# A graph layer's routed messages in two float32r parts in place of three bf16 parts

## The reference

```python
h = x @ W_in2f
Wij = ssp(f_ij @ W_filt1 + b_filt1) @ W_filt2 + b_filt2     # ssp(v) = softplus(v) - ln 2
Wij = Wij * rcut_ij[:, None]
x_ij = h[idx_j] * Wij                                       # idx_j is dst
agg = segment_sum(x_ij, idx_i, num_segments=6250)           # idx_i is src, in no order
out = ssp(agg @ W_out1 + b_out1) @ W_out2 + b_out2
return layernorm(x + out)
```

## Time and profile before

| | |
|---|---|
| runs | 2374.13, 2367.33, 2362.75 us; median 2367.33 |
| span of the profiled execution | 2368.4 us, the only time given for it |
| PE / DVE / ACT / POOL busy | 2142.1 / 1670.5 / 1660.6 / 1862.0 us |
| PE matmul instructions | 16313 |
| granted TensorE clock, mean | 0.964 |
| DMA moved | 250.00 MB |
| chain that ended last, by engine | DMA 43%, PE 19%, POOL 17%, issue 14% |

### The profile page before, as it was taken

The page is one execution under the profiler, slowest core; times in us unless marked ns, Lnnn a source line. Parts: engine busy times, 40 slices in busy tenths (PEclk is TensorE's granted clock), DMA queues, the critical chain, the costliest instruction groups (busy, mean ns, idle before and its releaser), DMA issues.

```text
span 2368.4 us, 60320 instructions
## 1 busy us (share of the span) xinstructions
PE 2142.1 (90%) x16313; PEld 1410.6 (60%) x16313; DVE 1670.5 (71%) x3879; ACT 1660.6 (70%) x3725; POOL 1862.0 (79%) x1174
## 2 busy tenths in 40 slices
PE   2488999999999999999999999999999999999936
PEld 1365666566666666666666566666666666666613
DVE  5467777768676777767777777777777777777726
ACT  0277777678687777777776777877777777777616
POOL 2078888888888888888888888888888888888874
PEclk8599999999999999999999999999999999999978
DMA  6776665666666666666666666656666566666574
GB/s 208 267 155 95 96 95 90 93 90 100 94 99 92 100 97 95 92 98 97 93 98 93 94 94 94 102 94 96 96 98 91 93 100 95 95 96 91 68 159 130
DMA packets 370945, 250.00 MB, mean 106 GB/s; under 512 B 88788, under 2 KB 350143, under 8 KB 370315
## 3 DMA queue, kind: packets, MB, share of 16 engines
q0 software_dynamic: 160560, 73.14, 32.7%
q1 hardware_dynamic: 199482, 155.27, 27.3%
q10 hardware_dynamic: 10476, 16.77, 1.9%
HBM read 149.90 MB, written 95.13 MB: 103 GB/s over the span
## 4 chain that ended last, share of the span: by engine, by line
DMA 43%; PE 19%; POOL 17%; issue 14%; DVE 3%; ACT 3%; POOLq 0%; SPq 0%; DVEq 0%; ACTq 0%
DMA table<-total,index 40%; POOL table L732 16%; PE unit_psum L1872 5%; PE unit_psum L1891 4%; PE both_psum L1828 3%; PE total_psum L1841 2%; PE pre_psum L1815 2%; DMA h_parts<-h_out 1%; DMA src_g<-in_src 1%; PE both_psum L1853 1%; PE both_psum L1824 1%; ACT out_rows L1122 1%; DVE rank L1249 0%; DVE rank_part L1244 0%; POOL half_sum L776 0%
## 5 line engine op out<-in xcount | busy, mean ns | idle before, releaser
L732 POOL DMA_INDIRECT table<-total,index x1115 | 1803.3, 1617 | 444.8 <-issue 249.0
L1872 PE MATMUL unit_psum<-moving,route_hot 128*128 128x386 bf16 x3136 | 608.8, 331 | 41.0 <-ACT ring L915 36.9
L885 ACT ACTIVATE h_dst<-both_psum,cols 128x128 f32<-128x128 f32 x1564 | 450.2, 386 | 102.4 <-PE both_psum L1853 99.0
L1891 PE MATMUL unit_psum<-scat_hot,ring 64*128 64x448 bf16 x4704 | 481.7, 353 | 9.2 <-DVE scat_hot L1432 6.5
L1872 PEld LDWEIGHTS unit_psum<-moving,route_hot 128*128 128x128 bf16 x3136 | 295.0, 99 | 266.9 <-ACT ring L915 108.2
L915 ACT ACTIVATE ring<-unit_psum 128x386 bf16<-128x386 f32 x784 | 373.5, 509 | 111.8 <-PE unit_psum L1872 70.5
L1828 PEld LDWEIGHTS both_psum<-w_f,hidden 128*128 128x128 f32 x3128 | 415.3, 193 | 18.3
L1828 PE MATMUL both_psum<-w_f,hidden 128*128 128x128 f32 x3128 | 415.7, 276 | 0.0
L1891 PEld LDWEIGHTS unit_psum<-scat_hot,ring 64*128 64x128 bf16 x4704 | 217.0, 95 | 218.5 <-DVE acc_t L1448 7.7
L849 ACT ACTIVATE soft<-pre_psum 128x1024 f32<-128x1024 f32 x196 | 201.9, 1030 | 169.5 <-PE pre_psum L1815 168.6
L1841 PE MATMUL total_psum<-message,same 128*128 128x129 f32 x2232 | 309.5, 281 | 4.8 <-DVE message L1360 4.3
(11 more groups left out here) (116 smaller groups left out, 1599.7 us busy)
## 6 DMA issues: line engine op xcount, KB each, us to landing
dst_b<-dst SPq DMA_DIRECT2D x391, 128.0 KB
src_b<-src SPq DMA_DIRECT2D x279, 128.0 KB
f_t<-in_f_t SPq DMA_DIRECT2D x98, 256.0 KB
table<-total,index POOLq DMA_INDIRECT x1115
table<-zeros ACTq DMA_DIRECT2D x20, 640.0 KB, 5.7
window<-h_parts SPq DMA_DIRECT2D x391, 32.0 KB
parts<-table SPq DMA_DIRECT2D x48, 256.0 KB, 5.2
h_parts<-h_out SPq DMA_DIRECT2D x12, 384.0 KB, 5.4
```

The costliest lines, as they stand in the source:

```text
L732: pool.indirect_dma_start(tables[table], bass.IndirectOffsetOnAxis(index[:, i, k:k + 1], 0), total[:, i, k, 0:DIM], None, compute_op=ALU.a ...
L885: last = act.activation(h_dst[:, b, d], source, ACT.Copy, scale=cols[:, g[1] // HALF % 2, weight:weight + 1])
L1872: last = pe.matmul(unit_psum[:, k % 2, 0:MOVING], route_hot[:, tile, k * P:(k + 1) * P], moving[:, tile, :], start=(tile == 0), stop=(tile ...
L1891: last = pe.matmul(unit_psum[:, strip, 0:BUCKET], ring[rows, r[1] % RING, slot_tile(m), part * DIM:(part + 1) * DIM], scat_hot[rows, r[1] ...
```

## The change

The routed messages go in two float32r parts. [...] So `take_rest`, `split_mid` and `slot_nodes` go, `split_lo` subtracts `moving`'s first part from the message, and the node number travels as one float32r beside a zero. `MOVING` is 258 columns where it was 386. `ring`, `scat_hot`, `route_hot` and `moving` are float32r and take more room, so four buffers lie in the space of `x_rows`. Therefore x's rows are loaded when the last message is made and the last routing matmul is through, and VectorE waits for the zeroed tables before its first group. The order of the other calls stays as it is.

```diff
-MOVING = 3 * DIM + 2
+MOVING = 2 * DIM + 2
...
-        local_parts = sb("local_parts", [P, ROUTES, TILES, 2], BF16)
-        slot_node = sb("slot_node", [P, RING, SLOT_TILES], F32)
+        local_cols = sb("local_cols", [P, ROUTES, TILES, 2], F32)
...
-        ring = at(0, "ring", [P, RING, SLOT_TILES, MOVING], BF16)
-        scat_hot = at(37856, "scat_hot", [P, RING, BUCKET], BF16)
-        route_hot = at(44128, "route_hot", [P, TILES, SLOT_ROWS], BF16)
-        moving = at(51296, "moving", [P, TILES, MOVING], BF16)
-        message_r = at(54400, "message_r", [P, TILES, DIM], F32)
-        rest_r = at(56448, "rest_r", [P, TILES, DIM], F32)
+        ring = at(0, "ring", [P, RING, SLOT_TILES, MOVING], F32R)
+        scat_hot = at(50592, "scat_hot", [P, RING, BUCKET], F32R)
...
+        def before_x(offset, name, shape, dt):
+            return nc.alloc_sbuf_tensor_at(name, shape, dt, offset=x_rows_at + offset)
+
+        route_hot = before_x(0, "route_hot", [P, TILES, SLOT_ROWS], F32R)
+        moving = before_x(14336, "moving", [P, TILES, MOVING], F32R)
+        message_r = before_x(18464, "message_r", [P, TILES, DIM], F32)
+        h_dst = before_x(20512, "h_dst", [P, 2, GROUP], F32)
...
             def load_rows_of_x():
                 full = FULL_CHUNKS * CHUNK
-                sp.wait_ge(tables_zeroed, ZEROED)
+                sp.wait_ge(message_done, GROUPS)
...
-                if is_at(g, 2 * QUAD):
-                    load_rows_of_x()
...
             with sp.If(is_narrow):
                 run_groups(sp, step_narrow)
+                sp.wait_ge(route_mm_done, through_tile((0, ROUTES - 1), SLOT_TILES - 1))
+                load_rows_of_x()
                 for k in range(TABLES):
                     sp.wait_ge(table_added[k], adds_before((0, GROUPS - 1), plain, tiles_in((0, GROUPS - 1)), k))
...
-                act.activation(moving[:, :, 3 * DIM:MOVING],
-                               local_parts[:, bass.ds(PER_UNIT * r[0] + r[1], 1), :, :]
+                act.activation(moving[:, :, 2 * DIM:MOVING],
+                               local_cols[:, bass.ds(PER_UNIT * r[0] + r[1], 1), :, :]
                                .rearrange("p a k c -> p (a k) c"), ACT.Copy).then_inc(local_done, 1)
-
-            def split_mid(r):
...
-                dve.tensor_copy(local_parts[:, :, :, 0], nodes).then_inc(meta_step, 1)
+                dve.tensor_copy(local_cols[:, :, :, 0], nodes).then_inc(meta_step, 1)
                 steps += 1
-                dve.wait_ge(meta_step, steps)
-                dve.tensor_tensor(local_parts[:, :, :, 1], nodes, local_parts[:, :, :, 0], ALU.subtract
-                                  ).then_inc(meta_step, 1)
+                dve.memset(local_cols[:, :, :, 1], 0.0).then_inc(meta_step, 1)
...
                         dve.wait_ge(hi_done, through_routed(plus(r, -1)))
-                        dve.wait_ge(rest_done, through_routed(plus(r, -1)))
+                        dve.wait_ge(lo_done, through_routed(plus(r, -1)))
...
-            def take_rest(r):
...
-                dve.wait_ge(mid_done, through_routed(r))
-                dve.wait_ge(rest_done, through_routed(r))
-                dve.tensor_tensor(moving[:, :, 2 * DIM:3 * DIM], rest_r[:, :, :], moving[:, :, DIM:2 * DIM],
+                dve.wait_ge(hi_done, through_routed(r))
+                dve.tensor_tensor(moving[:, :, DIM:2 * DIM], message_r[:, :, :], moving[:, :, 0:DIM].bitcast(F32),
                                   ALU.subtract).then_inc(lo_done, 1)
...
-            def slot_nodes(r):
...
-                dve.wait_ge(node_done, through_routed(r))
+                dve.wait_ge(ring_done, through_tile(r, SLOT_TILES - 1))
...
-                                  slot_node[:, r[1] % RING, k:k + 1], None, ALU.is_equal).then_inc(hot_done, 1)
+                                  ring[:, r[1] % RING, k, 2 * DIM:2 * DIM + 1].bitcast(F32), None, ALU.is_equal
+                                  ).then_inc(hot_done, 1)
...
-                slot_nodes(r(-2))
                 finish_hidden(pair(1))
-                take_rest(r(-1))
+                split_lo(r(-1))
                 slot_one_hot(m(0), 6)
                 multiply(g(1), plain)
-                split_lo(r(-1))
...
             with dve.If(is_narrow):
+                dve.wait_ge(tables_zeroed, ZEROED)
                 run_units(dve, unit, rest)
...
+                    if is_at(c, 0):
+                        dve.wait_ge(x_rows_loaded, 32)
...
-                    pe.wait_ge(mid_done, through_routed(r))
...
-                for part in range(3):
+                for part in range(2):
                     for strip in range(STRIPS):
...
-                                         stop=final and part == 2)
+                                         stop=final and part == 1)
```

More of the change, by code:

```diff
@@ L76 @@
 assert LAST_UNIT < GROUPS <= LAST_UNIT + 7
-F32, BF16 = mybir.dt.float32, mybir.dt.bfloat16
+F32, BF16, F32R = mybir.dt.float32, mybir.dt.bfloat16, mybir.dt.float32r
 I32, U16 = mybir.dt.int32, mybir.dt.uint16
@@ L467, in build @@
         acc_zeroed = sem("acc_zeroed")
-        hi_done, rest_done, mid_done, lo_done = (sem(n) for n in ("hi_done", "rest_done", "mid_done", "lo_done"))
+        hi_done, lo_done = sem("hi_done"), sem("lo_done")
         local_done, route_hot_done, route_mm_done = sem("local_done"), sem("route_hot_done"), sem("route_mm_done")
-        ring_done, node_done, hot_done = sem("ring_done"), sem("node_done"), sem("hot_done")
+        ring_done, hot_done = sem("ring_done"), sem("hot_done")
         taken_done, acc_done = sem("taken_done"), sem("acc_done")
@@ L1411, in route_one_hot @@
                     hot.then_inc(route_hot_done, 1)
-            def slot_nodes(r):
-                if not routes(r):
-                    return
-                dve.wait_ge(ring_done, through_tile(r, SLOT_TILES - 1))
-                dve.tensor_tensor(slot_node[:, r[1] % RING, :], ring[:, r[1] % RING, :, 3 * DIM],
-                                  ring[:, r[1] % RING, :, 3 * DIM + 1], ALU.add).then_inc(node_done, 1)
             def slot_one_hot(m, x):
@@ L1488, in unit @@
                 route_one_hot(r(0), 2); route_one_hot(r(0), 3)
-                take_rest(r(0))
-                slot_nodes(r(-1))
+                split_lo(r(0))
                 slot_one_hot(m(1), 6)
                 finish_hidden(pair(3))
-                split_lo(r(0))
                 multiply(g(5), plain)
@@ L1512, in unit @@
                 compare_dst(g(10))
-                slot_nodes(r(0))
-                take_rest(r(1))
+                split_lo(r(1))
                 slot_one_hot(m(2), 6)
@@ L1540, in unit @@
                 multiply(g(11), plain)
-                take_rest(r(2))
-                slot_nodes(r(1))
+                split_lo(r(2))
                 compare_dst(g(14))
@@ L1565, in unit @@
                 route_one_hot(r(3), 0); route_one_hot(r(3), 1); route_one_hot(r(3), 2); route_one_hot(r(3), 3)
[L1566 to L1567 removed]
+                split_lo(r(3))
                 multiply(g(15), plain)
                 slot_one_hot(m(4), 6)
[L1570 removed]
                 mark_repeated(g(14), plain)
@@ L1591, in unit @@
                 multiply(g(18), plain)
-                take_rest(r(4))
-                slot_nodes(r(3))
+                split_lo(r(4))
                 compare_dst(g(21))
                 slot_one_hot(m(5), 6); slot_one_hot(m(6), 0); slot_one_hot(m(6), 1)
-                split_lo(r(4))
                 slot_one_hot(m(6), 2)
@@ L1616, in unit @@
                 compare_dst(g(24))
-                slot_nodes(r(4))
-                take_rest(r(5))
+                split_lo(r(5))
                 slot_one_hot(m(6), 6)
```

40 lines of the change are left out of this document (5 added, 35 removed).

## The result

The kernel after the change took 2394.35 us (median; 2387.63 to 2398.10), the kernel before, on the same chip, 2365.04. The ratio is 1.0112, with an interval of 1.0093 to 1.0132: slower, by more than the 0.5% that a measurement can tell from no change. The forecast was 2374 in a range from 2345 to 2405. The profiled execution's span is 2391.7 us against 2368.4, +23.3.

The account below looks back on a forecast made before the run. POOL's scatters were taken to bound the kernel: 19.3 (one-hots) - 8.4 (take_rest) - 5.6 (waits) + 1.4 (x's rows) = +6.7 us on 2367.3, forecast 2374. The range was 2345 to 2405, and 2353 to 2395 from its own bounds.

Parts of the forecast that it names:

- POOL paces the loop: Loop: POOL's 1115 scatters run one after the other, 0.30 us apart; PE, DVE and ACT wait for it through buffers.
- The one-hots' length: VectorE: float32r output lengthens slot one-hots by 58 ns and route one-hots by 170 ns, +122 us of DVE.
- The price of the growth: Scatters: blocking weight is count x duration squared, 0.160 us a unit; longer one-hots add 120.3 units, +19.3 us.
- take_rest's -8.4: VectorE: dropping take_rest removes blocking weight 52.2, so scatters shorten by 8.4 us.
- Waits of 5.6 us that would close: Gaps between scatters: a PE that catches up sooner closes POOL's real waiting, -5.6 us.
- x's rows: Late load of x's rows, near the last scatters: the same 1.4 us as now, bounds 0 and +3.
- TensorE's saving: Slot and route matmuls: float32r streams as bf16 does, saving 325 us over 112 intervals, none on the path except 5.6 us.
- the rival at 2615: Matmuls: float32r runs at float32's rate a column, 336 us more PE, so PE becomes the bound; chance 0.07.
- The slower one, 2398: Scatters: only the one-hot form blocks POOL, so one-hots cost +35 us and take_rest gives nothing; chance 0.20.
- The faster one: VectorE: float32r output takes one-hots to one element a step, no longer blocking, -40.3 us on POOL, 2323; chance 0.08.

Follow-up runs that it names:

- e10: Kernel before with only the 784 slot one-hots read from padded odd rows (7 rows of 64): 2349.47 us, ratio 0.9915.
- e11: Kernel before with only the 448 route one-hots read from padded odd rows: 2369.53 us, ratio 1.0001.
- e2: Kernel before with all one-hots read and written as seven rows over a padded source: 2400.18 us, ratio 1.0134.
- e1: Kernel before with the one-hots' source row of node numbers in float32 instead of uint16, output still bf16: 2455.24 us, ratio 1.0357.
- e7: Kernel after with all one-hots in seven rows over a padded source: 2765.84 us, ratio 1.1666 to the kernel before.
- e5: Kernel before with an unread extra product on VectorE ahead of each of 391 multiplies, one input in PSUM: 2395.63 us, ratio 1.0110.
- e12: e1 without take_rest and split_mid, copies and route matmuls 258 columns wide, 42 bf16 slot matmuls kept (second part counted twice): 2394.18 us, ratio 1.0094.
- e3: Kernel before with x's rows loaded only when the last message is made: 2370.48 us, ratio 1.0000.
- e4: Kernel before with an unread extra product on VectorE ahead of each of 391 multiplies, both inputs in SBUF: 2407.96 us, ratio 1.0177.
- e9: Kernel after with the second part's slot matmuls issued twice, 42 as before: 2387.60 us, ratio 1.0074 to the kernel before.
- e6: Kernel before with the first part's slot matmuls alone, 14 an interval in place of 42: 2377.40 us, ratio 1.0031.
- e8: e1 with the first part's slot matmuls alone, 14 in place of 42: 2614.77 us, ratio 1.1049 to the kernel before.

## Why the prediction was right and wrong

The span grew by 23.3 us where the sum had 6.7. Of the 16.6 between, 11.4 are the scatters (+22.3, where the sum had 19.3 - 8.4) and 5.7 the gaps (+1.5, where it had -5.6 + 1.4). The time stayed in the range, close to the 2395 that the text's own bounds reach.

**POOL paces the loop: right.** The +23.3 us of span are +22.3 of scatters, +1.5 of gaps, +0.1 at the start and -0.6 behind the last scatter. TensorE's 146 us less in the loop gave nothing.

**The one-hots' length: the term that was mis-sized.** The step took 385 ns of the earlier trace rows whole, and added 0.521 ns an element to it. The slope was right: after's medians, 681 and 444, are 0.529 ns an element apart. The fixed part was not: 385 - 448 x 0.521 = 152 ns in that row, 444 - 448 x 0.529 = 207 ns in after. The kernel's own one-hots had shown it: 327 and 448 ns give 0.27 an element and 206 ns fixed. With that part the step would have read 440 and 673. The row compares with a constant, the one-hots with a column of scalars; that this is the cause of the 55 ns is likely, and was not tried alone. By the means the growth was +231 and +112 ns where the sum had +170 and +58.

**The price of the growth: right in sum by luck, wrong in form.** With the measured means the weights grow by 122.6 + 71.7 = 194.3; times 0.160 is 31.1, less 8.4 for take_rest 22.7, and 22.3 were measured. Its terms don't come out: by the count, what scatters that asked during a slot one-hot hold over 1540 ns went from 5.1 to 28.9 us, +23.8, where 71.7 x 0.160 is 11.5, and under split_lo, which the sum took as unchanged, from 23.4 to 12.8. The same law misses the other runs by up to 16 us: e10's 97.1 units gave 28.9 us, 0.30 each, e11's 101.9 gave 23.5, e2's 199.0 gave 47.5, while e1's 190.9 more cost 20.9, 0.11 each. Busy time (count times mean) fits these better: e10 276 us, 0.105 us each; e11 214 us, 0.110; e2 490 us, 0.097; e1 +188 us, 0.111; e7 -681 us, 0.081. By this measure after's +191 us of one-hots are +19 us, less some 8 for take_rest's 76.5, so it falls short of the 22.3 in turn. The square needs requests that fall at random and holds that end with the instruction; e5 and e10 show that neither holds. What would replace it is open. take_rest's -8.4 was never tried alone: e12, which drops it and more from e1, has 2.9 us less of scatters than e1.

**Waits of 5.6 us that would close: wrong.** The excess is 7.1 us. Of the kernel before's 5.6, 2.8 are two gaps 12 us behind a turn of the loop, which a lighter TensorE doesn't end.

**x's rows: right, about nothing.** e3 shows no cost. In after the load stands at 2264.5 us, and two gaps behind it, 1.93 and 0.96 us where 0.30 is usual, hold 2.3 us against the 1.4 taken.

**TensorE's saving: half of what was said, off the path.** 325 us were expected. The route matmuls went from 608.8 to 528.6 us busy and the slot matmuls from 481.7 to 388.7, 173 together. The chain of work of after, dense stretches beside the earlier trace rows:

```profile
1177.86 0.47 PE unit_psum L1824 x4
...
1179.46 3.06 PE unit_psum L1843 x28
```

3.06 / 28 is 0.109 us a slot matmul against 4.08 / 42 = 0.097; 0.47 / 4 is 0.118 for 258 columns against 0.165 for 386. Float32's rate, as the text had it, would be 0.224 and 0.389 us. So float32r doesn't run at it, which ends the rival at 2615, but each instruction costs more than its columns. The weight loads doubled, from 99 to 198 ns by the mean. Here the forecast took columns alone. The Trainium skill (FP8 and Floating Point Precision, TensorE Precision Notes) has true FP32 as four passes and, beside it, a reduced form that reads 4 bytes and truncates them; it doesn't name float32r. The trace agrees with the prediction's reading that float32r is that cheaper form: 0.118 us for 258 columns is 0.46 ns a column, against 0.43 in bf16.

**The rivals.** The slower one, 2398, came within 4 us of the time and is still wrong as a mechanism: it wants an instruction with two SBUF inputs to hold nothing, and e4 shows that it does. The faster one, one element a step for float32r output, needs a median near 1200 ns for a route one-hot; it is 681. e7 shows what it would have done: not 2323, but 2766, as VectorE became the bound, which its own text had called close.

**The step that the text did not have.** It said that a lighter TensorE and ScalarE give nothing, since POOL paces. What a relief can give is the lead that absorbs the loop's turns. The same one-hots without it cost 65.7 us of gaps (e1: 71.3 against 5.6). Of the change, taking out the third part's chain paid for that (e12); dropping a third of the slot matmuls did not (e9), and by e6 and e8 fewer matmuls rather cost, likely through the clock.

## What to carry to other kernels

Where one queue paces a loop, price an edit twice: by what it does to one instruction of that queue, and by what it does to the lead of the engines that feed it, read from how long they wait for the pacing queue (134.7 us before, 24.2 in the version that opened gaps), because regular stalls such as a loop's turn are paid by that lead. It is a warning and no law: e8's 26.4 us is no less than e1's, with gaps of 246 us against 71. For the cost of a changed operand type take only the slope from a foreign row, and the fixed part from the instruction's own rows. And on VectorE look for the form that doesn't hold the other queue before looking for the shortest form: 784 instructions made 85 ns longer gave 0.85%.

## What the runs showed of the hardware

- A one-hot of 448 elements took 327 ns (uint16 to bf16), 444 (uint16 to float32r), 442 (float32 to bf16) by the median, and held scatters in each case; in seven rows over a padded source it took 436 ns, and scatters that asked during it took 1542 ns by the mean. With float32r output the odd rows cost 672 ns.
- A hold ends with the instruction only if none follows at once that holds too: scatters that asked during split_lo took 1991 ns by the mean in the kernel before, and 1683 in e10, where the slot one-hots behind it hold nothing.
- TensorE's granted clock was lower in the versions where it had less to do: mean in the loop 0.99 before, 0.95 after, 0.94 in e6, 0.90 in e8. e8 is 160 us slower than e1, with 28 slot matmuls fewer in each interval; that the clock is the cause is likely and not shown.
- A turn of the hardware loop stopped TensorE for 2.5 us by the mean in the kernel before (32.5 / 13), up to 4.3 us in e1, with no engine waited for.
- A float32r weight load took 198 ns by the mean against 99 in bf16, and a dense float32r matmul of 448 columns 0.109 us against 0.097.
